# Three down projections and a residual moved at the hand-over from feed-forward to attention

## What is computed

```python
x = x + 0.5 * ffn(layernorm(x), W_up, W_gate, W_down)
x = x + attn(layernorm(x), Wq, Wk, Wv, Wo, head_scale)
x = x + 0.5 * ffn(layernorm(x), W_up, W_gate, W_down)
# ffn: silu(x @ wu.T) * (x @ wg.T) @ wd.T, 1024 hidden, weights made ternary
# attn: 16 query heads, 4 key/value heads of 128, rotary, causal softmax
```

## Time and profile before

| | us |
|---|---|
| median of 3 runs | 1089.22 (1087.47 to 1089.34) |
| profiled execution | 1088.83 |
| its span, first to last instruction | 1087.0 |
| PE busy | 1069.8 (98%) |
| DVE busy | 923.1 (85%) |
| ACT busy | 815.8 (75%) |
| POOL busy | 715.1 (66%) |

### The profile page before, as it was taken

How to read it: one execution, slowest core, us unless ns; L and a number is a source line. 1 busy time by engine, 2 the same in 40 slices (tenths; PEclk the granted TensorE clock), 3 DMA queues, 4 the chain that set the end, 5 groups by cost and what they waited for, 6 DMA issues and landing times.

```text
span 1087.0 us, 26892 instructions
## 1 busy us (share of the span) xinstructions
PE 1069.8 (98%) x8517; PEld 844.5 (78%) x8517; DVE 923.1 (85%) x2313; ACT 815.8 (75%) x2038; POOL 715.1 (66%) x906
## 2 busy tenths in 40 slices
PE   8999999999999999999999999999999999999998
PEld 5556566788888888888888888888888887566665
DVE  6787886899999999999999999999999997433333
ACT  6787997787888788887877878778787785444443
POOL 2566675777777777777777777777777774444443
PEclk9999999999999999999999999999999999999999
DMA  9522332234434343344333443334334343100101
GB/s 348 155 49 40 58 59 40 45 74 93 70 74 82 71 83 68 72 82 79 76 68 72 82 82 72 76 72 83 74 72 82 72 82 69 30 19 19 39 19 39
DMA packets 262166, 79.93 MB, mean 74 GB/s; under 512 B 249328, under 2 KB 260848, under 8 KB 261872
## 3 DMA queue, kind: packets, MB, share of 16 engines
q1 hardware_dynamic: 261696, 79.19, 35.1%
q10 hardware_dynamic: 432, 0.27, 0.1%
HBM read 12.85 MB, written 4.19 MB: 16 GB/s over the span
## 4 chain that ended last, share of the span: by engine, by line
PE 74%; issue 10%; POOL 6%; ACT 5%; DVE 4%; DMA 0%; POOLq 0%; DVEq 0%; ACTq 0%
PE bank L759 45%; PE bank L818 14%; POOL SCR L428 6%; PE bank L718 5%; PE bank L728 5%; PE bank L748 4%; ACT SCR L628 1%; DVE ARENA L1144 1%; ACT ARENA L635 1%; PE bank L677 1%; DVE SCR L962 1%; DVE bank L1168 1%; ACT SCR L502 0%; DVE X L952 0%; ACT SCR L517 0%
## 5 line engine op out<-in xcount | busy, mean ns | idle before, releaser
L453 POOL TENSOR_SCALAR SCR<-SCR,RI 128x128 f32<-128x128 f32 (+1 forms) x512 | 311.1, 608 | 44.2 <-DVE RI L1140 4.1
L628 ACT ACTIVATE SCR<-bank,NM 128x128 f32<-128x128 f32 (+1 forms) x512 | 208.5, 419 | 122.8 <-DVE NM L1168 122.7
L418 POOL TENSOR_TENSOR SCR<-SCR 128x512 f32<-128x512 f32 x160 | 203.4, 1271 | 146.0 <-DVE SCR L962 144.6
L428 POOL TENSOR_TENSOR SCR<-SCR 128x512 f16<-128x512 f32 x128 | 151.4, 1185 | 154.1 <-ACT SCR L517 152.0
L818 PE MATMUL bank<-SCR 128*128 128x128 f32 (+1 forms) x1024 | 193.7, 332 | 4.4 <-ACT SCR L628 3.3
L523 ACT COPY SCR<-bank 64x512 f32<-64x512 f32 x320 | 185.6, 580 | 14.2 <-PE bank L759 8.1
L981 DVE SCALAR_TENSOR_TENSOR SCR<-SCR,CS,bank 128x512 f32<-128x512 f32 x128 | 95.1, 743 | 115.9 <-PE bank L728 103.5
L1144 DVE TENSOR_TENSOR ARENA<-SCR,ARENA 128x768 f16<-128x768 f32 x128 | 186.7, 1459 | 4.8 <-ACT ARENA L635 3.9
L759 PE MATMUL bank<-WOH,ARENA 128*128 128x256 f16 x1024 | 188.3, 273 | 0.8 <-DVE X L1177 0.8
L1168 DVE CUSTOM_DVE_ANT_0 bank<-bank,MASK,SCQ 128x128 f32<-128x128 f32 (+1 forms) x512 | 182.8, 415 | 3.5 <-PE bank L818 2.7
L534 ACT ACTIVATE SCR<-bank,SU 128x512 f32<-128x512 f32 x128 | 87.7, 685 | 110.7 <-PE bank L718 110.5
(11 more groups left out here) (120 smaller groups left out, 1649.1 us busy)
## 6 DMA issues: line engine op xcount, KB each, us to landing
out<-X SPq DMA_DIRECT2D x7, 512.0 KB, 2.9
X<-in_x SPq DMA_DIRECT2D x1, 2560.0 KB, 11.2
ARENA<-in_wq SPq DMA_DIRECT2D x1, 2048.0 KB, 13.9
ARENA<-in_wo SPq DMA_DIRECT2D x1, 2048.0 KB, 18.8
SCR<-ARENA SPq DMA_TRANSPOSE x128, 3.6
X<-in_x SPq DMA_DIRECT2D x3, 512.0 KB, 9.9
X<-in_wu SPq DMA_DIRECT2D x2, 512.0 KB, 5.6
X<-in_wg SPq DMA_DIRECT2D x2, 512.0 KB, 7.4
```

What stands on the lines that cost most here:

```text
L418: gp.tensor_tensor(dst, M1[:, m, :], M2[:, m, :], ALU.add).then_inc(add, 1)
L428: gp.tensor_tensor(HL[layer][:, f % 4, :], H32[layer][:, f % 2, :], HH[layer][:, f % 4, :], ALU.subtract).then_inc(s["hl_done"], 1)
L453: last = gp.tensor_scalar(EX[:, par, lo:hi], EX[:, par, lo:hi], RI[:, par, c:c + 1], PS, ALU.mult, ALU.mult)
L628: last = act.activation(EX[:, par, 384 * hh + lo:384 * hh + hi], SBK[hh][:, lo:hi], ACT.Exp, bias=NM[:, par, c:c + 1], scale=-1.0, accum_o ...
```

## The change

On PE, in batch 0, down 5 is put behind the projection of step 1, and so ahead of the scores of step 0. Downs 6 and 7 are put right behind those scores, ahead of the projection of step 2. Before, down 5 stood behind the projection of step 2, down 6 behind the scores of step 1, and down 7 behind the scores of step 2. On DVE the residual of the last tile is put ahead of the rotation of step 2; it stood behind the rotation of step 4. No instruction is added or taken away.

```diff
@@ -860,6 +860,8 @@
                     if first and i == 2:
                         pe.wait_ge(ff[0]["h_done"], FC * TILES)
                         scores(0, 0, 0)
+                        down(0, TILES - 1, FC - 2)
+                        down(0, TILES - 1, FC - 1)
                     if real(b, i, 0) and not (first and i == 0):
                         r, m = 5 * u + 1 + k, (5 * g + 1 + k) % 2
                         if k == 0:
@@ -869,10 +871,10 @@
                         if first and i in (1, 2):
                             pe.wait_ge(ff[0]["silu_done"], FC * TILES - 2 + i)
                         project_qk(PJ[m], WQH, WQL, 8 * g + 2 * k, b)
+                        if first and i == 1:
+                            down(0, TILES - 1, FC - LAG)
                     if real(b, i, 2) and not (first and i == 2):
                         scores(t - 2, (i - 2) % PAIRS, unit(2))
-                    if first and 2 <= i < 2 + LAG:
-                        down(0, TILES - 1, FC - LAG + i - 2)
                     if isinstance(b, int) and b == BATCH:
 
                         for pair in {2: (2, 3), 3: (4,), 4: (5,)}.get(i, ()):
@@ -1124,10 +1126,10 @@
                         maxima(t - 2, i % 2)
                     if early and i == 1:
                         maxima(0, 0)
+                    if isinstance(b, int) and (b, i) == (0, 2):
+                        residual(0, TILES - 1)
                     if real(b, i, 0) and not first:
                         rope_mul(r, m, PJ[m])
-                    if isinstance(b, int) and (b, i) == (0, 4):
-                        residual(0, TILES - 1)
                     if real(b, i, 6):
                         ve.wait_ge(oh, t - 5)
                         h = 2 * ((i - 6) % PAIRS) * SEQ
```

## The result

Over 20 runs each, the kernel before has a median of 1088.87 us (1087.47 to 1090.00) and the changed one 1090.25 us (1088.96 to 1091.51). The ratio is 1.0013, with a 95% interval of 1.0007 to 1.0019: some 0.8 to 2.1 us slower, a difference that is there but under 0.2% by its middle. 1090.31 had been forecast. The lowest runs of the two kernels, in which TensorE's clock is least likely to have fallen, are 1087.47 and 1088.96, 1.49 us apart.

A forecast was written before the change was run, and what follows sets the result against it. A ring of ACT and DVE was taken to set the end from 191.5 to 263 us. Downs 6 and 7 add 1.74 us, the residual's removal returns 0.26: 1088.83 + 1.48 = 1090.31 us, range 1088.3 to 1092.0.

The forecast's parts named there:

- Down 5 in the gap: PE ahead of the first scores: 0.87 us of matmuls fit into 0.98 us idle for POOL, costing nothing.
- the ring: ACT and DVE, 191.5 to 263 us: maxima, exponentials, high cast and low part in turn set the end, not PE.
- Downs 6 and 7, 1.74 us: PE, between first scores and projection of step 2: 16 matmuls delay swap, rotation and maxima of step 2 by 1.74 us.
- The residual hidden: DVE ahead of the third rotation: its 1.57 us lie in idle time, about 0.8 us to spare, costing nothing.
- Case C: Rival, DVE: residual not hidden, third rotation waits up to 1.57 us more; 3.05 us slower, 1091.88 us; chance 0.10.
- What its removal gives back, 0.26 us: DVE before the maxima of step 3: removing the residual returns 0.26 of 1.74 us, leaving them 1.48 us later.
- The bounds, 0.92 and 1.74: Limits of the shift at the maxima of step 3: 0.92 us if L1144 is short, 1.74 if nothing is given back.
- The lag stays: From step 3 to the values at 262.99 us: queue orders are unchanged, so the 1.48 us lag persists.
- Case B: Rival, steps between 207 and 262 us: a wait takes up the 1.48 us, time stays 1088.8 us; chance 0.10.
- Case A, PE as the pace: Rival: PE sets the pace everywhere, so filled waits of 0.87 and 0.66 us count; 1087.30 us; chance 0.12.
- PE's catching up: PE after the moved downs: it only stands idle longer ahead of the scores of steps 1 and 3, awaiting ACT's exponentials.
- the base of the sum, 1088.83: Time of the profiled execution before the change, 1088.83 us, to which the 1.48 us shift was added.

The follow-up runs named there:

- The dose of three downs: Changed kernel with down 5 also between the scores of step 0 and the projection of step 2, 24 matmuls instead of 16: 1090.70 us, ratio 1.0021.
- the one with the residual left: Changed kernel with the residual kept behind the rotation of step 4, as before the change: 1090.03 us, ratio 1.0013.
- the 22 runs of the two kernels: Kernel before with identity matmuls in both early PE gaps, 1087.75 us; the same with POOL's add for the first query rotation moved ahead, 1086.88 us.

## Why the prediction was right

Each step, with 1.42 us added to the times of after for its early start:

- **Down 5 in the gap.** Forecast: idle time of 0.1 us left, nothing on the path. Measured: 188.64 to 188.76, 0.12 us, and down 5 moved alone changed the ring by 0.02.
- **Downs 6 and 7, 1.74 us.** The projection of step 2 was forecast at 191.88 and is at 191.89; the third rotation 194.67 and 194.67; the maxima of step 2 203.64 and 203.64. The dose of three downs confirms the price, 0.86 for one more.
- **The residual hidden.** About 0.8 us was to be left; 0.77 was. Case C, in which it delays the rotation, did not occur.
- **What its removal gives back, 0.26 us.** Measured 0.27, as the distance between the changed kernel and the one with the residual left. L1144 was forecast at 207.02 with 1.48 us, and is at 207.01 with 1.48; the maxima of step 3 at 208.43, and are at 208.42. The bounds, 0.92 and 1.74, were the cases of no contention and of nothing given back; the second is what the kernel with the residual left shows (19.93 - 18.19 = 1.74). That L1144 is long when POOL's add reads at the same time is now seen in both directions and at several overlaps: 1.48 us with 0.67 us of overlap, 1.27 with 0.45, 0.97 with 0.15, 0.92 with none. So all but 0.1 us of the overlap is lost, however long it is, and the next instruction of DVE starts 0.74 us behind the end of the add each time (at 207.00, 200.10 and 201.08 us of their traces). A sharing by halves would have lost half the overlap. The lock of the Trainium skill, SBUF — State Buffer, section Who interferes with whom, agrees with it.
- **The lag stays.** The values that wait for the DMA were forecast at 264.5 and are at 264.45. Case B, a lag that is taken up, did not occur: it is 1.47 us at the maxima of step 3 and 1.46 at the values.
- **Case A, PE as the pace.** It would have made the kernel 1.5 us faster. By it down 5 alone should have gained 0.87 us and gained 0.02 in the trace, and the three downs should have been at 1088.9 us or less and were at 1090.7. In this stretch PE is no busier than DVE (52.09 and 52.13 of 56.00 us); the 98% is that of the whole.

Two things were not as written. PE's catching up was to show as idle time ahead of the scores of steps 1 and 3 only; 1.24 us of it lies ahead of the projection of step 5, which waits until DVE has emptied the bank (L964). It changes nothing, since the ring does not wait for that projection. And the base of the sum, 1088.83, was a profiled execution in which the clock had fallen; the median of 20 runs, 1088.87, happened to be the same. That 1090.31 lies within 0.1 us of 1090.25 is therefore in part luck; what the mechanism gives is the shift, forecast as 1.48 us, 1.46 in the traces and 1.38 between the medians.

## What to carry to other kernels

A gap on the busiest engine is worth only as much as what it delays. Ask first which engines set the end of that stretch; filling a gap of PE while a ring of ACT and DVE sets the pace gave 0.02 us, and work put ahead of an instruction that feeds the ring cost its full length. Work taken off the ring gives back not its length but the distance to what is late next, here 0.27 of 1.57 us. Where traces differ by less than their early microseconds do, measure distances from a common instruction instead of comparing spans.

## What the runs showed of the hardware that was not expected

Single runs of one kernel lie up to 2.9 us apart (1087.02 to 1089.90 over 31 runs of before). The profiled ones show much of it: the granted clock between 15 and 25 us was 1.00 and 1.00 in one and 0.76 and 0.90 in another, where the four matmuls of a gate projection took 1.70 us at 19.69 instead of 1.03. The idle times of PE ahead of it were 0.89 and 1.94 us in the execution in which it fell, and 1.00 and 1.82 us in the one in which it did not. So the length of these gaps alone does not decide it. With both filled, the 22 runs of the two kernels lie within 0.76 and 0.65 us, and the clock of none is under 0.999. What makes it fall in one run and not in the next stays open.
